# Projection of a gated attention block: first rows in halves, the next rows' turn, the rounding of the first weights and the last values moved

## The reference

```
xn = (x - mean) / sqrt(var + 1e-5)            # 4 x 1024 rows of 256
qkv = xn @ w_qkv                              # 256 -> 3 * 256
q, k, v = qkv[.., 0] / 4, qkv[.., 1], qkv[.., 2]
s = softmax(causal(q @ k^T)) @ v @ w_out
for i in range(6):
    y = gelu(y @ W1[i]^T + b1[i]) @ W2[i]^T + b2[i] + y     # y starts as xn; layer norm between the blocks
out = x + s * silu(y)
```

## Time and profile before

| | us |
|---|---|
| median of three runs | 1561.3 (1560.0 to 1563.26) |
| the profiled execution, its own time | 1562.57 |
| its span, first to last instruction | 1560.6 |
| PE busy in the span | 1535.3 (98%) |
| DVE busy | 1220.2 (78%) |
| ACT busy | 958.0 (61%) |
| POOL busy | 386.2 (25%) |
| mean granted TensorE clock | 0.999 of full |

### The profile page before, as it was taken

One profiled execution on the slowest core, in us unless ns is written; L12 is line 12 of the kernel. 1 busy time (PEld: TensorE's weight loads), 2 busy tenths in 40 slices (PEclk: granted clock), 3 DMA queues, 4 the chain that ended last, 5 costly groups with the idle time before them and its releaser, 6 DMA issues. The chain is left out here.

```text
span 1560.6 us, 28823 instructions
## 1 busy us (share of the span) xinstructions
PE 1535.3 (98%) x11004; PEld 1204.0 (77%) x11004; DVE 1220.2 (78%) x2689; ACT 958.0 (61%) x1404; POOL 386.2 (25%) x325
## 2 busy tenths in 40 slices
PE   8999999999999999999999999999999999999998
PEld 7888888888888888888888888888888744444443
DVE  7845988889888898888898888988676577777742
ACT  3445565555655555655556555555445599898986
POOL 1102322222222222222222222231101132333333
PEclk9999999999999999999999999999999999999999
DMA  8969547457455114142141341130720355566441
GB/s 291 321 219 237 151 123 195 128 142 191 122 130 125 52 52 116 48 107 68 41 115 49 65 115 49 55 103 29 201 67 28 96 153 163 149 186 180 116 124 55
DMA packets 110418, 193.38 MB, mean 124 GB/s; under 512 B 13660, under 2 KB 81244, under 8 KB 102620
## 3 DMA queue, kind: packets, MB, share of 16 engines
q1 hardware_dynamic: 110280, 191.54, 43.6%
HBM read 136.70 MB, written 79.95 MB: 139 GB/s over the span
## 5 line engine op out<-in xcount | busy, mean ns | idle before, releaser
L776 ACT ACTIVATE m_hid<-m_h_ps,m_b1s 128x512 f32<-128x512 f32 x384 | 264.7, 689 | 486.7 <-PE m_h_ps L880 435.3
L852 DVE TENSOR_TENSOR m_hidl<-m_hid,m_hidh 128x512 fp32r<-128x512 f32 x384 | 353.4, 926 | 185.3 <-ACT m_hidh L779 175.9
L1112 ACT ACTIVATE a_prob<-a_st_ps 128x1024 f32<-128x1024 f32 x288 | 277.6, 1023 | 35.2 <-PE a_st_ps L1183 30.3
L893 PE MATMUL m_y_ps<-shared,m_hidh 128*128 128x256 f32 x1536 | 274.0, 281 | 2.0 <-DVE xres L811 1.9
L779 ACT ACTIVATE m_hidh<-m_h_ps,m_b1s 128x512 fp32r<-128x512 f32 x384 | 261.6, 681 | 0.0
L880 PE MATMUL m_h_ps<-xth,shared 128*128 128x512 f32 x768 | 254.5, 392 | 2.6 <-PEq L296 1.7
L893 PEld LDWEIGHTS m_y_ps<-shared,m_hidh 128*128 128x128 f32 x1536 | 235.4, 188 | 19.0 <-issue 9.6
L893 PE MATMUL m_y_ps<-w2h,m_hidh 128*128 128x256 f32 x768 | 218.6, 285 | 1.8 <-DVE xres L811 1.8
L893 PE MATMUL m_y_ps<-shared,m_hidl 128*128 128x256 f32 x768 | 212.9, 277 | 0.0
L893 PE MATMUL m_y_ps<-w2l,m_hidh 128*128 128x256 f32 x768 | 212.9, 277 | 0.0
L893 PE MATMUL m_y_ps<-w2h,m_hidl 128*128 128x256 f32 x768 | 212.8, 277 | 0.0
(11 more groups left out here) (122 smaller groups left out, 2546.8 us busy)
## 6 DMA issues: line engine op xcount, KB each, us to landing
turned_rows<-apart SPq DMA_DIRECT2D x47, 512.0 KB, 2.7
apart<-turned_rows SPq DMA_DIRECT2D x188, 128.0 KB, 3.1
mq<-q_stacks SPq DMA_DIRECT2D x16, 896.0 KB, 7.2
mk<-k_stacks SPq DMA_DIRECT2D x16, 896.0 KB, 10.7
shared<-k_stacks SPq DMA_DIRECT2D x14, 896.0 KB
shared<-q_stacks SPq DMA_DIRECT2D x14, 896.0 KB
q_stacks<-q_parts SPq DMA_DIRECT2D x96, 128.0 KB
k_stacks<-k_parts SPq DMA_DIRECT2D x96, 128.0 KB
```

Of the source, the lines that this page charges most:

```text
L776: nc.scalar.activation(hid[n % 2][:], h_ps[n % 2][:], ACT.Gelu, bias=b1s[i % 2][:, k:k + 1])
L852: nc.vector.tensor_tensor(hidl[n % 4][:], hid[n % 2][:], hidh[n % 4][:].bitcast(F32), ALU.subtract).then_inc(low_done, 1)
L893: m = nc.tensor.matmul(y_ps[:, j, :], h[n % 4][:, j * P:(j + 1) * P], w[par][:, k, :], start=(k == 0 and j % 2 == 0 and h is hidh and w is ...
L1112: nc.scalar.activation(to, scores, ACT.Exp).then_inc(exp_done, 1)
```

## The change

Six edits, all in `project`:

1. The first group's rows are turned in halves into two separate halves of `tr_ps`, each with its own signal; `high0` and `low0` handle 256 rows each, in a 128 x 2 x 256 view.
2. The first result is made in another order (`first_queries`): the four products with `gth` first, waiting for both high halves and the weights, then the two with `gtl`. `keep_awake` counts go from 16 and 12 to 20 and 5.
3. `NEXT_ROWS_AT`: in groups 0 and 1 the next group's rows are turned behind the fourth result, ahead of the values; in the others between queries and keys as before. Group 0's DVE order is written out apart, with `statistics(1)` ahead of `split_w(2)`.
4. The first weights: ACT rounds the piece (`high_piece`) and DVE only subtracts (`low_piece`); the pieces go to groups 1 to 7 (`PIECES_AT`), two of them to group 6.
5. The last group's values are made between its queries and keys.
6. SP reloads pieces by `PIECES_AT`.

```diff
+        PIECES_AT = {1: (0,), 2: (1,), 3: (2,), 4: (3,), 5: (4,), 6: (5, 6), 7: (7,)}
+        NEXT_ROWS_AT = [4, 4] + [2] * (GROUPS - 3)
...
-            def first_weights(g):
-                dve.wait_ge(piece_loaded[g % 2], 32 * (g // 2 + 1))
-                split_piece(nc, dve, keep, 0, g, piece_high, g + 1).then_inc(piece_split, 1)
+            def first_weights(piece):
+                dve.wait_ge(piece_high, piece + 1)
+                low_piece(nc, keep, 0, piece).then_inc(piece_split, 1)
...
             split_w(0)
-            low(0)
+            low0(0)
+            low0(1)
             split_w(1)
+            statistics(1)
             split_w(2)
-            statistics(1)
-            for g in range(GROUPS):
+            norm(1)
+            for m in range(3):
+                split_low(0, m)
+            low(1)
+            statistics(2)
+            split_low(0, 3)
+            for g in range(1, GROUPS):
                 if g + 1 < GROUPS:
                     norm(g + 1)
...
+            def first_weights(piece):
+                act.wait_ge(piece_loaded[piece % 2], 32 * (piece // 2 + 1))
+                high_piece(nc, keep, 0, piece).then_inc(piece_high, 1)
...
                 if g < GROUPS - 1:
                     values(g)
+                    for piece in PIECES_AT.get(g, ()):
+                        first_weights(piece)
...
+            def first_queries():
+                pe.wait_ge(w_split, 1)
+                pe.wait_ge(high0_done, 2)
+                products = [(w, c, gth) for c in range(HALVES) for w in (wh, wl)] + [(wh, c, gtl) for c in range(HALVES)]
+                for order, (w, c, t) in enumerate(products):
+                    if order == 2 * HALVES:
+                        pe.wait_ge(low0_done, 2)
...
-            keep_awake(16)
+            keep_awake(20)
             transpose0()
-            keep_awake(12)
-            pe.wait_ge(w_split, 1)
+            keep_awake(5)
             for g in range(GROUPS):
-                pe.wait_ge(low_done, g + 1)
-                if g == GROUPS - 1:
-                    values(g)
+                if g:
+                    pe.wait_ge(low_done, g)
                 queries_keys(g)
+                if g + 1 < GROUPS and NEXT_ROWS_AT[g] == 4:
+                    transpose(g + 1)
                 if g < GROUPS - 1:
                     values(g)
```

More of the change, by code:

```diff
@@ L329, in project, with first_ps @@
         WCOLS = [slice(DIM * part, DIM * (part + 1)) for part in range(3)]
+        FIRST_TOKENS = [slice(GT // 2 * part, GT // 2 * (part + 1)) for part in range(2)]
+        PIECES_AT = {1: (0,), 2: (1,), 3: (2,), 4: (3,), 5: (4,), 6: (5, 6), 7: (7,)}
+        NEXT_ROWS_AT = [4, 4] + [2] * (GROUPS - 3)
+        def first_ps(part):
+            return tr_ps[:, part, :].rearrange("p (c n) -> p c n", c=HALVES)
         block = ctx.enter_context(nc.Block())
@@ L359, in _ @@
                 store_values(g)
-                if g + 2 < GROUPS:
-                    sp.wait_ge(piece_split, g + 1)
-                    weight_piece(sp, keep, w1t, w2t, 0, g + 2, piece_loaded)
+                for piece in PIECES_AT.get(g, ()):
+                    if piece + 2 < CH:
+                        sp.wait_ge(piece_split, piece + 1)
+                        weight_piece(sp, keep, w1t, w2t, 0, piece + 2, piece_loaded)
             sp.wait_ge(v_copied, GROUPS)
@@ L414, in low @@
             def low(g):
-                dve.wait_ge(high_done, g + 1)
+                dve.wait_ge(high_done, g)
                 if g >= 2:
@@ L418, in low, with low0 @@
                 nc.vector.tensor_tensor(gtl[g % 2][:], tr_ps[:], gth[g % 2][:].bitcast(F32), ALU.subtract).then_inc(low_done, 1)
+            def low0(part):
+                tokens = FIRST_TOKENS[part]
+                dve.wait_ge(high0_done, part + 1)
+                nc.vector.tensor_tensor(gtl[0][:, :, tokens], first_ps(part), gth[0][:, :, tokens].bitcast(F32), ALU.subtract).then_inc(low0_done, 1)
             def split_low(g, m):
@@ L465, in _ @@
                 if g == GROUPS - 1:
-                    first_weights(g)
+                    for piece in PIECES_AT[g]:
+                        first_weights(piece)
                 split_low(g, 0)
@@ L481, in high @@
             def high(g):
-                act.wait_ge(transposed, g + 1)
+                act.wait_ge(transposed, g)
                 if g >= 2:
@@ L485, in high, with high0 @@
                 nc.scalar.activation(gth[g % 2][:], tr_ps[:], ACT.Copy).then_inc(high_done, 1)
+            def high0(part):
+                act.wait_ge(transposed0, part + 1)
+                nc.scalar.activation(gth[0][:, :, FIRST_TOKENS[part]], first_ps(part), ACT.Copy).then_inc(high0_done, 1)
+            def first_weights(piece):
+                act.wait_ge(piece_loaded[piece % 2], 32 * (piece // 2 + 1))
+                high_piece(nc, keep, 0, piece).then_inc(piece_high, 1)
             def part0(g, m):
@@ L506, in _ @@
             high_w(0)
-            high(0)
+            high0(0)
+            high0(1)
             high_w(1)
@@ L511, in _ @@
                 if g == GROUPS - 1:
-                    values(g)
-                part0(g, 0)
-                part0(g, 1)
-                if g + 1 < GROUPS:
+                    for piece in PIECES_AT[g]:
+                        first_weights(piece)
+                for m in range(4):
+                    if m == 2 and g == GROUPS - 1:
+                        values(g)
+                    if g + 1 < GROUPS and m == NEXT_ROWS_AT[g]:
+                        high(g + 1)
+                    part0(g, m)
+                if g + 1 < GROUPS and NEXT_ROWS_AT[g] == 4:
                     high(g + 1)
-                part0(g, 2)
-                part0(g, 3)
                 if g < GROUPS - 1:
                     values(g)
+                    for piece in PIECES_AT.get(g, ()):
+                        first_weights(piece)
         @block.tensor
@@ L528, in transpose0 @@
                     pe.wait_ge(normed0, part + 1)
-                    for j in range(TILES)[tiles]:
+                    for t, j in enumerate(range(TILES)[tiles]):
                         for c in range(HALVES):
-                            i = nc.tensor.transpose(tr_ps[:, c, j * P:(j + 1) * P], xres[:, j, c * P:(c + 1) * P], ident[:])
-                i.then_inc(transposed, 1)
+                            i = nc.tensor.transpose(first_ps(part)[:, c, t * P:(t + 1) * P], xres[:, j, c * P:(c + 1) * P], ident[:])
+                    i.then_inc(transposed0, 1)
             def transpose(g):
                 pe.wait_ge(normed, g)
-                pe.wait_ge(low_done, g)
+                if g == 1:
+                    pe.wait_ge(low0_done, 2)
+                else:
+                    pe.wait_ge(low_done, g - 1)
                 for c in range(HALVES):
@@ L540, in transpose @@
                 i.then_inc(transposed, 1)
+            def first_queries():
[4 more added lines that the diff above has]
+                    if order == 2 * HALVES:
+                        pe.wait_ge(low0_done, 2)
+                    i = nc.tensor.matmul(qk_ps[0][:], w[:, c, 0:P], t[0][:, c, :], start=(order == 0), stop=(order == len(products) - 1))
+                i.then_inc(qk_done, 1)
             def queries_keys(g):
@@ L544, in queries_keys @@
                 for m in range(4):
-                    if m == 2 and g + 1 < GROUPS:
+                    if g + 1 < GROUPS and m == NEXT_ROWS_AT[g]:
                         transpose(g + 1)
+                    if m == 2 and g == GROUPS - 1:
+                        values(g)
+                    if g == 0 and m == 0:
+                        first_queries()
+                        continue
                     if g:
```

1 line of the change is left out of this document (added).

## The result

The change takes 1564.78 us (median of 17 runs, 1562.06 to 1569.05) against 1561.59 for the kernel before on the same chip (17 runs): ratio 1.0019, 95% interval [1.0012, 1.0027]. That is 3.2 us or 0.2% slower, small, clear of noise, and at the line that the prediction drew between "no change" and "slower" (1564.4, or 1564.7 from this median); the forecast was 1562.8, the range 1557.0 to 1567.0. The profiled execution took 1565.55 (span 1563.7) against 1562.57 (1560.6).

A forecast was written before the change was run, and what follows sets the result against it. PE, busy 98% of the span, was taken as the bound, so only its pauses and clock could be won. -5.95 + 6.5 + 0.25 + 0.65 = +1.45 on the profiled 1562.57 gave 1564.0, a median of 1562.8; range 1557.0 to 1567.0.

The forecast's parts named there:

- Front: Start of `project`: first rows in halves and later next rows let PE start group 1 at 18.84 against 24.79, gaining 5.95.
- E(0): Time when PE has finished group 0's values and could start the next group: forecast 18.84 against 24.79 before.
- New wait: Turns of groups 3 to 7: DVE's subtractions wait for ACT's roundings behind its values copy; five pauses of 1.3, +6.5.
- E(6): Time when PE has finished group 6's values and could start the next group: forecast 80.06 against 79.51 before.
- End of the stage: Last group of `project`: ACT waits for piece 7, landing taken as 2.9; MLP starts 11.8 after group 6's values, +0.25.
- Clock: MLP's start: PE pauses 3.4 instead of 1.68, clock falls, up to 0.9 returns at the fourth slot; +0.65.
- a covered wait: Rival, 14%: PE's turns come late anyway or ACT's chain is shorter than 2.75; without the 6.5, 1556.3.
- a late last piece: Rival, 17%: ACT waits for piece 7 ahead of the last queries, landing 5.4 after issue instead of 2.9; 1566.2.
- a fall of the clock in the pauses: Rival, 6%: the five pauses of 1.3 lower the clock at 1.6 each, 8 more; 1570.8.
- a lost early gain: Rival, 3%: statistics or DMA hold group 1 as before and the pauses merge with that; about 1561.
- The chance for "slower", 0.25: Whole kernel above 1564.4: 0.06 + 0.13 + 0.06, against 0.59 for within 0.2% and 0.16 for faster.
- the bounds of the landing and the clock: End of `project` and MLP's start: landing 2.3 to 5.4 gives -0.35 to +2.75; the clock's cost 0 to 1.6.

## Why the prediction was right

The forecast (no change, 1562.8) named the mechanism and nearly every time in `project`. The total is less well met: the median came out 2.0 above the forecast, the change itself 3.1 in the profiles where 1.45 was summed, and the range, 10 us wide, covered a loss that no step had. Step by step:

- **Front, -5.95.** Measured -5.83. The first result came at 9.16 instead of 9.56, since the clock rose in the middle of the first transposes (the first four start 0.21 apart, the last 0.11; before all eight 0.21). But the turn stayed at 15.2, as DVE sets it: its statistics began 0.4 earlier than counted, and POOL's power took 1.38 where 1.01 was assumed, with 0.90 of DVE's wait for it uncovered. The two errors cancel, by luck: 15.20 for 15.22 at the turn, 18.96 for 18.84 at E(0). The clock's stretch at 0.50 is gone, as forecast.
- **New wait, five of 1.3, +6.5.** Measured: spacing 10.42, thus 1.30 each, and 61.38 from E(0) to E(6) against the 54.72 of six groups before, +6.66. The turn comes at E + 3.98 (28.18 to 32.16), where the sum of the chain had 4.0 to 4.1. Undoing it and doing it alone both gave its price. Not foreseen: with the rounding on DVE 0.58 of the pause ahead of group 3's turn is there as well, so that moving it to ACT cost there only the rest. The chain of copy, roundings, subtractions, normalisation stands in the rows link by link.
- **End of the stage, +0.25.** Measured -0.05: SP's second load at E + 3.1, landing 2.6 instead of 2.9, values stored at E + 8.4 instead of 8.9, MLP at E + 11.5 instead of 11.8. The row of the median had 3.9. The Trainium skill (DMA: Bandwidth & Descriptors, Anatomy of one DMA — SWDGE (gpsimd) path) gives an estimate of 2.3; the measured 2.6 on a nearly empty queue is nearest to the page, though the page fitted its figures to DMAs that GpSimd issues, and SyncE issues this one. With E(6) late by 0.3 more than forecast, the MLP's start is right to 0.02.
- **Clock, +0.65.** The level fell as said, after a pause of 3.09 (3.4 forecast); it cost 1.49 at the first slot, and 0.62 instead of 0.9 came back at the fourth slot, whose wait shrank to 0.28 from the 0.90 of the earlier trace rows: +0.87. That is the term that was mis-sized, by 0.2, on the return.
- **What no step had**: +1.45 behind the third slot, 1.24 of it at slot 26. It comes from the landing of four loads; no instruction there was edited. The profile of the change has the step at 1.2 and its second one at 0.7. Whether the change shifts these loads against each other, or the kernel before was lucky in its one profile, stays open: the other versions have it smaller or reversed, and no run took the stacks' loads away.

Term by term, -5.83 + 6.66 - 0.05 + 0.87 + 1.45 = +3.1, the difference of the two spans. Without the last term it would be 1.65, where 1.45 was forecast. The rivals: a covered wait is refuted by the five pauses, a late last piece by the landing of 2.6, a fall of the clock in the pauses by a clock of 1.00 from 15 to 92.8, with five pauses of 1.02 to 1.07 in it, a lost early gain by E(0). The chance for "slower", 0.25, took most of its mass from the bounds of the landing and the clock; the time came out at that edge, for a reason that was not among them.

## What to carry to other kernels

An engine with much idle time is not a free place for work that others wait for: what counts is what stands ahead of the work in its queue, here a copy that waits for PE. The same two instructions cost 1.3 us per group behind the copy and made no pause over 0.3 ahead of it, so list for each moved instruction what its engine does last before it and who waits behind the consumer. Where an edit with several parts moves a time little, measure the parts: this one held 6 us of gain (0.4%) from parts that work, spent by one that doesn't.

## What the runs showed of the hardware

TensorE's clock fell after some pauses and not after others. After pauses of 1.1 and 1.7 us, and after five of 1.05 in a row, it stayed at 2.4 GHz (granted 1.00). Pauses of 2.54, 2.55, 2.75, 2.89, 3.04 and 3.09 were each followed by some 3.4 us at 1.2 GHz (granted 0.50; 92.9 to 96.3 in the change), at a cost of 1.5 to 1.65 where it could be read. The fall could come after PE was back at work: in the change PE multiplied from 91.84 to 92.84 at 1.00. No run has a pause between 1.72 and 2.54 once PE has begun. The Trainium skill (TensorE: Matmul & The Clock Gate, Why this matters for your kernels) warns of gaps above about 3 us. The trace disagrees by a little: the bracketed pauses are some 0.25 short of the real ones (1.05 for a loss of 1.30), so the shortest was about 2.8, an estimate, and it cost as much as those above 3.

Four DMAs of 128 KB issued behind two of 896 KB landed 11.6 us after their issue in the kernel before (median of the four), 13.0 and 12.9 in the two profiles of the change and 11.7 to 12.6 in the others, with the order of the queue unchanged. Such a difference, nowhere near the edit, was 1.2 of the 3.1 us between the two profiles.
